# A fourth pipeline stage in a six-layer windowed-attention block, and a shorter reciprocal root

## What is computed

```python
for i in range(DEPTH):                      # DEPTH = 6
    x = attn_layer(shift_tokens(x), Wqkv[i], q_scale[i], k_scale[i], Wo[i]) + x
    x = ffn_layer(shift_tokens(x), ln_g[i], ln_b[i], W1[i], b1[i], W2[i], b2[i]) + x

def attn_layer(x, Wqkv, qs, ksc, Wo):       # 16 heads of 64, window 32
    q, k, v = split(x @ Wqkv)
    q, k = l2norm(q) * qs, l2norm(k) * ksc  # then rotary tables on q and k
    return local_attention(q, k, v) @ Wo    # softmax over 2 * 32 keys

def ffn_layer(x, g, bln, W1, b1, W2, b2):
    xn = (x - mu) / sqrt(var + 1e-5) * g + bln
    a, gate = split(xn @ W1 + b1)           # 2 x 341 columns
    return a * gelu(gate) @ W2 + b2
```

## Time and profile before

| | us |
|---|---|
| median of 3 runs | 4013.61 (4013.08 to 4021.07) |
| the profiled execution, its own time | 4012.41 |
| its span | 4010.5 |
| PE busy | 3607.0 (90%) |
| DVE busy | 3054.0 (76%) |
| ACT busy | 2344.9 (58%) |
| POOL busy | 1832.3 (46%) |
| weight loads (PEld) | 2732.1 (68%) |

### The profile page before, as it was taken

One profiled execution on the slowest core, in us unless ns is written; L12 is line 12 of the kernel. 1 busy time (PEld: TensorE's weight loads), 2 busy tenths in 40 slices (PEclk: granted clock), 3 DMA queues, 4 the chain that ended last, 5 costly groups with the idle time before them and its releaser, 6 DMA issues.

```text
span 4010.5 us, 161604 instructions
## 1 busy us (share of the span) xinstructions
PE 3607.0 (90%) x63907; PEld 2732.1 (68%) x63907; DVE 3054.0 (76%) x6212; ACT 2344.9 (58%) x4154; POOL 1832.3 (46%) x1604
## 2 busy tenths in 40 slices
PE   5858999998999998999999999998999998999996
PEld 2326777776777776777777777776777776777774
DVE  8986777786777777778777787787777777877873
ACT  1025666666666666666666666666666666666662
POOL 2435545544454444444444444444444444454541
PEclk9979999999999999999999999999999999999998
DMA  2004233233332333323324233233332232332332
GB/s 78 11 24 95 51 72 68 52 72 77 72 69 50 72 69 81 70 51 70 69 51 95 61 64 72 54 66 67 83 72 58 61 72 54 68 71 56 64 72 68
DMA packets 186330, 260.48 MB, mean 65 GB/s; under 512 B 31670, under 2 KB 89908, under 8 KB 185396
## 3 DMA queue, kind: packets, MB, share of 16 engines
q1 hardware_dynamic: 186164, 258.24, 29.5%
HBM read 22.30 MB, written 4.19 MB: 7 GB/s over the span
## 4 chain that ended last, share of the span: by engine, by line
DVE 43%; issue 22%; PE 21%; ACT 9%; DVEq 2%; POOL 1%; ACTq 1%; SPq 1%; DMA 0%; POOLq 0%
DVE ss L1148 9%; DVE ropec L1139 8%; DVE ropes L1140 7%; PE bank L732 5%; PE bank L631 4%; DVE mx L1186 4%; PE obank L681 2%; ACT L881 2%; DVE On L1202 2%; DVE bank L1176 2%; DVE bank L1178 2%; DVE rinv L1180 2%; ACT sq L826 1%; ACT gel L881 1%; DVE hm L1228 1%
## 5 line engine op out<-in xcount | busy, mean ns | idle before, releaser
L935 POOL TENSOR_TENSOR qn<-ropec,ropes 128x512 f32<-128x512 f32 x768 | 975.9, 1281 | 1370.9 <-DVE ropes L1140 1225.5
L941 POOL TENSOR_TENSOR qn<-qn,rinv 128x512 f32<-128x512 f32 x768 | 781.0, 1043 | 563.3 <-DVE rinv L1180 563.3
L826 ACT ACTIVATE sq<-bank 128x512 f32<-128x512 f32 x768 | 457.2, 595 | 355.6 <-PE bank L609 338.1
L1139 DVE TENSOR_TENSOR ropec<-bank,rots 128x512 f32<-128x512 f32 x768 | 524.3, 683 | 97.4 <-ACT sq L826 96.5
L631 PE MATMUL bank<-ident,qn 128*128 128x128 f32 x3072 | 483.8, 281 | 46.0 <-ACT qT L844 26.7
L1140 DVE TENSOR_TENSOR ropes<-bank,rots 128x512 f32<-128x512 f32 x768 | 523.1, 681 | 0.0
L1148 DVE TENSOR_REDUCE ss<-sq 128x8 f32<-128x512 f32 x768 | 503.8, 676 | 3.6 <-ACT sq L826 3.5
L631 PEld LDWEIGHTS bank<-ident,qn 128*128 128x128 f32 x3072 | 352.7, 142 | 206.1 <-POOL qn L941 86.4
L1228 DVE SCALAR_TENSOR_TENSOR hm<-bank,vec,gel 128x256 f32<-128x256 f32 (+1 forms) x288 | 139.1, 483 | 433.2 <-ACT gel L881 433.2
L607 PE MATMUL bank<-wqkv_hi,xs_hi 128*128 128x512 f32 x768 | 388.8, 506 | 61.3 <-DVE ropes L1140 25.5
L647 PEld LDWEIGHTS bank<-kT,qT 64*32 64x32 f32 x24576 | 359.9, 107 | 120.6 <-issue 120.6
(11 more groups left out here) (133 smaller groups left out, 6261.2 us busy)
## 6 DMA issues: line engine op xcount, KB each, us to landing
V<-Vt SPq DMA_DIRECT2D x576, 260.0 KB
V<-Vt SPq DMA_DIRECT2D x192, 130.0 KB
V<-Vt SPq DMA_DIRECT2D x192, 65.0 KB
xres<-X SPq DMA_DIRECT2D x96, 128.0 KB
X<-x SPq DMA_DIRECT2D x96, 128.0 KB, 3.6
wqkv_raw<-L_ffn_Wqkv SPq DMA_DIRECT2D x6, 1536.0 KB
xraw<-X SPq DMA_DIRECT2D x97, 64.0 KB, 2.0
xraw<-X SPq DMA_DIRECT2D x97, 63.8 KB, 1.9
```

The source lines that it names most:

```text
L826: act.activation(sq[:, c % 2, :], b_proj[n % 2][:], ACT.Square).then_inc(squared.sem, 1)
L935: pool.tensor_tensor(qn[:, c, :], ropec[:, c % ROPE_RING, :], ropes[:, c % ROPE_RING, :], ALU.add).then_inc(rope_sum.sem, 1)
L941: pool.tensor_tensor(heads8(qn[:, c, :]), heads8(qn[:, c, :]), rinv[:, 8 * c:8 * c + 8].unsqueeze(2).broadcast_to([P, 8, DH]), ALU.mult).t ...
L1139: dve.tensor_tensor(halves(ropec[:, c % ROPE_RING, :]), raw, table(t, 2 * kind), ALU.mult)
```

## The change

Three things change.

1. The FFN (`w1.0` to `w1.2`, `w2`, and SP's store of x2) of batch n-3 becomes a fourth stage with lag 3 (`'''`): it is taken up in the round after the one that made its xn. The pipeline has three rounds of filling and three of draining in place of two. Three rounds per layer change are written out in place of two. The FFN's weights are now converted in four steps instead of three, with a wait of its own for `w2`.
2. The reciprocal root of 66 columns takes 10 DVE instructions in place of 12. All but one wait for the one before: the two that both form the same product (one into SBUF, one into PSUM) are issued together.
3. The slot tables of PE, ACT, DVE and POOL are written in another order.

```diff
-NEWTON = 3
-RSQ_STEPS = 3 + 3 * NEWTON
+CUBIC = 0.375
+RSQ_STEPS = 10
...
-        pv.3'' tr.5' proj.0 tr.6' ot.2'' proj.1 tr.7' ot.3'' proj.2 qk.0' proj.3 proj.4 wo.0'' qk.1' proj.5
-        mean.0'' proj.6 qk.2' pt.0' proj.7 var.0'' pv.0' pt.1' qk.3' pt.2' pv.1' ot.0' ln.0'' pv.2' tr.0
-        w1.0'' tr.1 v.0 pt.3' v.1 w1.1'' v.2 tr.2 ot.1' w1.2'' tr.3 v.3 tr.4 w2.0'' """,
+        tr.0' pt.2'' w1.0''' pv.1'' proj.0 proj.1 tr.1' ot.0'' w1.1''' tr.2' pv.2'' pt.3'' tr.3' proj.2
+        proj.3 tr.4' ot.1'' w1.2''' tr.5' pv.3'' proj.4 ot.2'' tr.6' w2.0''' ot.3'' tr.7' proj.5 proj.6
+        qk.0' wo.0'' qk.1' proj.7 v.0 mean.0'' pt.0' qk.2' var.0'' pt.1' pv.0' qk.3' v.1 v.2 ln.0'' v.3 """,
...
             body(1, 0, (0,), 0, None)
             body(2, 1, (0, 1), None, None)
+            body(3, 2, (0, 1, 2), None, {2: 0})
             with eng.Fori(0, DEPTH - 1) as l:
                 loads and loads(l + 1)
-                with eng.Fori(2, NB) as g:
-                    body(l * NB + g + 1, g, (0, 1, 2), None, l)
+                with eng.Fori(3, NB) as g:
+                    body(l * NB + g + 1, g, (0, 1, 2, 3), None, {2: l, 3: l})
                 conv_a and conv_a(l + 1)
-                body(l * NB + NB + 1, 0, (0, 1, 2), l + 1, l)
-                body(l * NB + NB + 2, 1, (0, 1, 2), None, l, l + 1)
+                body(l * NB + NB + 1, 0, (0, 1, 2, 3), l + 1, {2: l, 3: l})
+                body(l * NB + NB + 2, 1, (0, 1, 2, 3), None, {2: l, 3: l}, (2, l + 1))
+                body(l * NB + NB + 3, 2, (0, 1, 2, 3), None, {2: l + 1, 3: l}, (3, l + 1))
...
-                if has_c:
-                    sp.wait_ge(c_x2.sem, c_x2.at(c, 1))
-                    sp.dma_start(X[:, place(wrap(g - 2))], x2[:]).then_inc(x_stored.sem, 16)
+                if has_d:
+                    sp.wait_ge(c_x2.sem, c_x2.at(n - 3, 1))
+                    sp.dma_start(X[:, place(wrap(g - 3))], x2[:]).then_inc(x_stored.sem, 16)
...
-                step(dve.tensor_scalar(rsq_t.bitcast(I32), rsq_x.bitcast(I32), 1, None, ALU.logical_shift_right))
+                step(dve.tensor_scalar(rinv[:].bitcast(I32), rsq_x.bitcast(I32), -0.5, RSQRT_SEED, ALU.mult, ALU.add))
+
                 wait()
-                step(dve.tensor_scalar(rinv[:].bitcast(I32), rsq_t.bitcast(I32), -1.0, RSQRT_SEED, ALU.mult, ALU.add))
-                for _ in range(NEWTON):
-                    wait()
-                    step(dve.tensor_tensor(rsq_t, rsq_x, rinv[:], ALU.mult))
-                    wait()
-                    step(dve.scalar_tensor_tensor(rsq_t, rsq_t, -0.5, rinv[:], ALU.mult, ALU.mult))
-                    wait()
-                    step(dve.scalar_tensor_tensor(rinv[:], rsq_t, 1.5, rinv[:], ALU.add, ALU.mult))
+                step(dve.tensor_tensor(rsq_t, rsq_x, rinv[:], ALU.mult))
+                wait()
+                step(dve.tensor_tensor(rsq_s[:], rsq_t, rinv[:], ALU.mult))
+                step(dve.tensor_tensor(rsq_y, rsq_t, rinv[:], ALU.mult))
+                wait()
+                step(dve.scalar_tensor_tensor(rsq_t, rsq_y, 10.0 / 3.0, rsq_s[:], ALU.subtract, ALU.mult))
+                wait()
+                step(dve.scalar_tensor_tensor(rinv[:], rsq_t, 5.0, rinv[:], ALU.add, ALU.mult))
...
```

More of the change, by code:

```diff
@@ L76, in fills @@
 def fills(*kinds):
-    return [(k, i) for lag in range(3) for k, i, g in order("pe") if g == lag and k in kinds]
+    return [(k, i) for lag in range(4) for k, i, g in order("pe") if g == lag and k in kinds]
 PROJ_ORDER = fills("proj", "v")
@@ L325, in run_slots @@
                 if kind == "wc":
-                    if next_c is not None:
-                        step(n - 2, next_c, i)
+                    if conv_c is not None and conv_c[0] == lag:
+                        step(n - lag, conv_c[1], i)
                     continue
                 if kind == "rsqrt":
-                    step(n, 0 in lags, 2 in lags)
+                    if 0 in lags or 2 in lags:
+                        step(n, 0 in lags, 2 in lags)
                 elif lag in lags:
@@ L488, in loads @@
                 hold(sp, sp_held, w_lo, 3 * layer)
-                hold(sp, sp_held, w_c, 3 * layer)
+                hold(sp, sp_held, w_c, 4 * layer)
                 load_weights(layer)
@@ L694, in c_wo @@
             def c_wo(c, _, layer):
-                pe.wait_ge(w_c, 3 * layer + 1)
+                pe.wait_ge(w_c, 4 * layer + 1)
                 pe.wait_ge(ot_copied.sem, ot_copied.at(c, 4))
@@ L725, in c_w1 @@
                 if j == 0:
-                    pe.wait_ge(w_c, 3 * layer + 3)
+                    pe.wait_ge(w_c, 4 * layer + 3)
                     pe.wait_ge(c_xn.sem, c_xn.at(c, 1))
@@ L733, in c_w1, with c_w2 @@
                 mm.then_inc(c_full.sem, 1)
-            def c_w2(c, _):
+            def c_w2(c, _, layer):
+                pe.wait_ge(w_c, 4 * layer + 4)
                 pe.wait_ge(c_h.sem, c_h.at(c, 3))
@@ L876, in c_w1 @@
                 if j == 0:
-                    act.wait_ge(w_c, 3 * layer + 3)
+                    act.wait_ge(w_c, 4 * layer + 4)
                 act.wait_ge(c_full.sem, c_full.at(c, 5 + j))
@@ L883, in c_ln_ @@
             def c_ln_(c, n, layer):
-                act.wait_ge(w_c, 3 * layer + 3)
+                act.wait_ge(w_c, 4 * layer + 2)
                 act.wait_ge(c_ln.sem, c_ln.at(c, 1))
@@ L900, in w_cs @@
                 elif k == 1:
+                    act.wait_ge(c_xn.sem, c_xn.at(c, 1))
+                    act.activation(vec[:, 0:2], vec_raw[:, 0:2], ACT.Copy).then_inc(w_c, 1)
+                elif k == 2:
                     act.wait_ge(c_full.sem, c_full.at(c, 7))
@@ L910, in w_cs @@
                     act.activation(vec[0:f2, 8:9], vec_raw[0:f2, 8:9], ACT.Copy).then_inc(w_c, 1)
-            for k in range(3):
+            for k in range(4):
                 w_cs(0, 0, k)
```

50 lines of the change are left out of this document (29 added, 21 removed).

## The result

| | before | changed | change with the store moved (first experiment) |
|---|---|---|---|
| median, us | 4013.44 | 4521.27 (4519.01 to 4524.13) | 3751.64 (3747.81 to 3756.47) |
| ratio to before, 95% interval | | 1.1261 [1.1241, 1.128] | 0.9345 [0.9329, 0.936] |
| span of the profiled execution | 4010.5 | 4518.4 | 3754.6 |
| PE / DVE / ACT / POOL busy | 3607 / 3054 / 2345 / 1832 | 3682 / 3147 / 2269 / 1851 | see the steady rounds below |

The changed kernel is 12.6% slower; the forecast was 3745 with a range up to 3865. The third column is the same kernel with one `if` in SP's program moved up.

The account below looks back on a forecast made before the run. PE, with 34.25 us of own work a round, was taken as the bound: 283.3 + 103 + 92 x 34.6 (3183) + 52 + 120 = 3741, forecast as a median of 3745 us, range 3675 to 3865.

Parts of the forecast that it names:

- paragraph on DMAs: SP's queue: V's last DMA issued at R (root done) + 22.6, x2's store behind it, all costed at nothing.
- slower side: PE, w1.0''' ahead of other slots: uncovered FFN handovers add 6.9 us, round 41.15, time 4348; chance 0.04.
- (a): Root-to-root loop of PE's own work without a wait: 34.25 us a round, the largest of three loops.
- (b): Loop through POOL's eight norms and seven adds, PE's tr.7' to qk.2', DVE's qk and the root: 33.0 us.
- (c): Loop through ACT and DVE at the round's head (exp, table load, gelu), then PE to qk.2' and root: 33.9 us.
- layer changes beyond them: At the five layer changes: 52 us in all, bounds 42.9 and twice that.
- The round: Steady round, 92 times: 34.6 us; forecast case 34.2 to 35.1, chance 0.58.
- open waits: PE waits left open at xn and at ot.0'' on the copy of pt.2'': 0.35 us a round.
- rival of tighter slots: PE with every group at 0.40: own work 33.5, (c) at 33.9 decides, round 34.0, time 3690; chance 0.15.
- Handovers of the FFN: Four handovers from root to x2 (2.0, 2.7, 1.1, 1.1 us) covered by PE work, except 0.2 to 0.4 at xn.
- The table load: On ACT: a switch costs 1.28 us and no more; both loops alike, 0.71 a round in 80 rounds within 34.6.
- The root: DVE's ten steps take 2.5 to 2.7 us, 0.5 to 0.7 less; worth nothing where PE is full, 0.6 elsewhere.

Follow-up runs that it names:

- fixed kernel: Changed kernel with SP issuing the store of x2 before the ten DMAs that place V: 3751.64 us, ratio 0.9345.
- 9: Fixed kernel with xs.0 at the head of ACT's table alone: 3717.12 us, ratio 0.9256.
- 11: Fixed kernel with xs.0 at the head of ACT's table and PE's tr.1' ahead of proj.0 and proj.1: 3718.68 us, ratio 0.9266.
- sixth experiment: Fixed kernel with xs.0 as the first slot of a round on both ACT and DVE: 3952.78 us, ratio 0.9857.
- 7: Fixed kernel with two weight conversions (wa.1, wa.2) moved later in ACT's and DVE's tables: 3757.0 us, ratio 0.9364.
- second experiment: Changed kernel with five of the ten V DMAs left out, the store still behind the rest: 3929.0 us (one execution).
- 5: Fixed kernel with the old twelve-step root put back: 3768.85 us, ratio 0.9396.
- 10: Fixed kernel with PE doing tr.1' ahead of proj.0 and proj.1: 3719.55 us, ratio 0.9262.

## Why the prediction was wrong

**The step that failed** stands in the paragraph on DMAs: "The store of x2 stands behind V, and its next user is a round later. All at nothing, under that cover". Both halves were read from the kernel before, where they held. A round later counts from the making of x2. What counts is the distance from the moment at which the queue gets to the store, and that moment hangs on pv.3'', since V's DMAs wait for it. The change moves pv.3'' from the head of the round to R + 14.5 (the prediction has that number) and the next x2 from the end of the round to just behind it. By the prediction's own terms the last DMA of V, and behind it the store, would be issued at R + 22.6, and w2.0''' on PE, behind pv.3'', a projection and two groups, ended at R + 14.5 + 0.79 + 2 x 0.44 + 1.46 = R + 17.6: a wait of 5.0 us and the landing of the store (3.7 in the trace) was there to be computed, 8.7 in all, and 7.69 came. The prediction asked of the queue whether V comes in time for ACT and not who waits for what stands behind V. It gave the slower side 0.04, and with another mechanism (handovers uncovered); that one didn't happen.

The loops (a), (b) and (c) were searched from root to root over PE, ACT, DVE and POOL only. The one that bound is a fourth: pv.3'' on PE, V on SP, the store, x2 on DVE, wo.0'' on PE, and through PE's slots back to pv.3'' of the next round. It passes SP's queue, which the walk left out. It does not pass the root: in the chain of waits PE goes on from wo.0'' (2047.29) to ln.0'' (2063.51) without a wait for it, as the root is done at 2063.08. From ln.0'' the chain takes DVE's lnt, ACT's xn and xs_hi and DVE's xs_lo to proj.0 (2067.86), and PE's own slots from there.

**The terms**, forecast, changed kernel, fixed kernel (us; spans):

| | forecast | changed | fixed |
|---|---|---|---|
| ahead of the rounds | 283.3 | 279.9 | 283.3 |
| first three intervals | 103 | 91.5 | 93.1 |
| 92 steady rounds | 92 x 34.6 = 3183 | 92 x 42.68 = 3926.6 | 92 x 34.33 = 3158.4 |
| layer changes beyond them | 52 | 78.7 | 94.9 |
| behind the last start | 120 | 141.7 | 125.0 |
| sum | 3741 | 4518.4 | 3754.7 |

With the store out of the way the remaining terms can be judged in the third column.

- *The round*: 34.33, within the forecast's 34.2 to 35.1, but by some luck. Its two parts were 34.25 of PE work and 0.35 of open waits; they measured 33.6 and 0.74, so the two errors went against each other. PE's work was that of the rival of tighter slots (33.5), though not by its reason. Groups of four take 0.43 to 0.44 as priced; it is the second of two projections (0.70 for 0.79), w1 (0.87 to 0.96 for 1.02) and w2 (1.31 for 1.46) that are shorter. That rival also has loop (c) deciding at 33.9, and 9 and 11 give 33.9 with PE waiting for ACT's head.
- *The open wait* was sought at xn and ot.0''. In the fixed kernel it was at xs_lo, for a reason given below; with that one gone it is at ot.0'' (0.27).
- *Handovers of the FFN*: covered. DVE stood 5.2 us for a gelu in the whole stretch 1000 to 4300 of the changed kernel, in 12 waits; before it was 335.6 in 226 from 1000 to 3880.
- *The table load*: 1.28 and no drain; nested and last loop alike, so the 0.7 between them is gone.
- *The root*: 2.5 (2.5 to 2.7 said), worth its full 0.68 in the old order and 0.14 net in the new one (0.6 and nothing said).
- *Loop (c)*: said to have 0.35 us of room. The sixth experiment put DVE's wait of 1.51 and xs_lo's 0.80 ahead of qk.3''; the round grew by 1.5, and by 1.6 more where the clock fell.
- *Layer changes*: mis-sized. 94.9 against 52, some 19 each where 10.4 were said, and above the upper bound of twice the old 42.9 (85.8). PE stands up to 6.3 us there for xs_lo behind the weight conversions, 3.3 for POOL's norms, and up to 2.9 for issue, and the clock falls to between 0.87 and 0.92 in two rounds of nearly every change. One part has the same reason as xs_lo below: DVE's conversion of 128x1024 (wqkv_lo, both inputs in SBUF) takes 2.06 us on the median in place of 1.22. Spreading two of the conversions (7) didn't help. What would is open.
- *First intervals, last batch*: 10 less and 5 more than said.

## What to carry to other kernels

An in-order DMA queue is an engine like the others: when a slot moves, walk the queue too. For every DMA ask when the queue reaches it in the new order, what the ones ahead of it wait for, and who reuses its source buffer next. A store that stands behind eight microseconds of issuing is free only as long as nobody wants its buffer back, and putting it first cost nothing here.

When PE falls idle for some microseconds, price the clock of the work behind it too: here it was 178 of 770 us. In the second experiment `wo` ran at the low clock behind a wait of 1.3 us in some rounds, and at the full one behind the same wait in others. And a wait can be too short to show as idle time: compare the start-to-start time of a slot with that of the same slot elsewhere, as with ot.0'' in 9 (0.70 and 0.43), before you call an engine full.

## What the runs showed of the hardware that was not expected

**A DVE instruction with both inputs in SBUF takes three times as long and more while POOL works.** xs_lo is 128x256, fp32, xraw minus xs_hi. Its durations (min/median/max ns) in the kernel before, the changed one, experiment 9:

```profile
L1129 DVE TENSOR_TENSOR xs_lo<-xraw,xs_hi x96: 415/426/428, 283.8 to 3889.4; 128x256 fp32r<-128x256 f32 x96
```

```profile
L1139 DVE TENSOR_TENSOR xs_lo<-xraw,xs_hi x96: 424/1311/1468, 280.4 to 4377.2; 128x256 fp32r<-128x256 f32 x96
```

```profile
L1139 DVE TENSOR_TENSOR xs_lo<-xraw,xs_hi x96: 424/791/1406, 281.2 to 3590.6; 128x256 fp32r<-128x256 f32 x96
```

Before, POOL was idle where xs_lo ran (from 2025.4 to 2032.95 in the round shown), in all 96. Now it runs its norms or adds there, for all but the first xs_lo. In the fixed kernel and in experiment 9, POOL's three norms and DVE's xs_lo:

```profile
1585.74 3.23 POOL L951 TENSOR_TENSOR qn<-qn,rinv 128x512 f32<-128x512 f32 x3
...
1586.76 1.30 DVE L1139 TENSOR_TENSOR xs_lo<-xraw,xs_hi 128x256 fp32r<-128x256 f32 x1 [0.41 <-ACT xs_hi L827]
```

```profile
1601.99 3.23 POOL L951 TENSOR_TENSOR qn<-qn,rinv 128x512 f32<-128x512 f32 x3
...
1602.53 0.79 DVE L1139 TENSOR_TENSOR xs_lo<-xraw,xs_hi 128x256 fp32r<-128x256 f32 x1
```

A third of 3.23 is 1.08, so the norms change over at about 1586.82 and 1587.89 in the one, at 1603.07 in the other. xs_lo ends 0.17 and 0.25 behind such a change, at 1588.06 and 1603.32: it looks as if DVE waits inside its own record until POOL's instruction is done. That reading agrees with the Trainium skill (page "SBUF — State Buffer", section "SBUF: two separate sides"), by which the two engines share a port pair that a DVE operation with two SBUF inputs and a GpSimd one hold for a whole instruction. The xs_lo of seven kernels (the changed and the fixed one, 5, 6, 9, 10 and 11) bear it out, taken by the time that POOL's running instruction, norm or add, still has to go when xs_lo starts:

| POOL still has, about, us | how many xs_lo | their median, us |
|---|---|---|
| 0.2 | 90 | 0.43 |
| 0.4 | 15 | 0.64 |
| 0.6 | 191 | 0.80 |
| 0.8 | 17 | 1.05 |
| 1.0 | 19 | 1.22 |

xs_lo ends some 0.2 us behind POOL's instruction. The 206 that start 0.08 us or less before such an end all run into the next instruction, and take 1.31 on the median. Since 0.2 is less than the 0.42 it takes alone, part of it seems to be done during the wait; how, no run here shows. No run moves POOL's work alone to test it. The rotary products, whose one input is in PSUM, kept their 0.68. So the 0.9 us that xs_lo lost went into the 0.66 us that PE waited in the fixed kernel, and starting it half a microsecond sooner (9) took that wait away, for 0.44 us a round.
